# Delta stage: decay sums of the first 16 chains issued one chain ahead of the key products, a second pair of banks for those products, and a denser order for the first batch of block inversions

## The reference, cut to what matters

```python
def step(S, x):
    qt, kt, vt, bt, gt = x
    S = S * jnp.exp(gt)[..., None, None]
    kv = jnp.einsum('bhk,ebhkv->ebhv', kt, S)
    delta = (vt[None] - kv) * bt[..., None]
    S = S + kt[None, :, :, :, None] * delta[..., None, :]
    ot = jnp.einsum('bhk,ebhkv->ebhv', qt * scale, S)
    return (S, ot)
```

## Time and profile before

| | |
|---|---|
| runs of the kernel before | 3254.01, 3258.17, 3269.35 us (median 3258.17) |
| span of the profiled execution | 3278.8 us; no separate device time of that execution is given, so its span stands for it |
| PE busy, DVE, ACT, POOL | 2990.0 (91%), 1674.9 (51%), 1128.2 (34%), 1485.6 (45%) us |
| mean granted TensorE clock | 0.943 of 2.4 GHz |
| delta stage, fronts alone | from 1340 us to 1452 us: 112 us, PE busy 69.91 us of it |
| delta stage, all parts and tail | from 1452 us to about 2000 us, PE busy 523.22 us of 548 |

### The profile page before, as it was taken

How to read it: one execution, slowest core, us unless ns; L and a number is a source line. 1 busy time by engine, 2 the same in 40 slices (tenths; PEclk the granted TensorE clock), 3 DMA queues, 4 the chain that set the end, 5 groups by cost and what they waited for, 6 DMA issues and landing times.

```text
span 3278.8 us, 46022 instructions
## 1 busy us (share of the span) xinstructions
PE 2990.0 (91%) x16081; PEld 1719.2 (52%) x16081; DVE 1674.9 (51%) x3820; ACT 1128.2 (34%) x2501; POOL 1485.6 (45%) x1471
## 2 busy tenths in 40 slices
PE   7999999888999899679999998998999999999828
PEld 3434566577676544357777765444533333444414
DVE  7633266588244432258777632442257777621361
ACT  3312422297122222345666332221034444332201
POOL 0565656498554457333333103554656666300003
PEclk9999999999999899859999778999999999999958
DMA  5400001210111244334554435211167666600404
GB/s 169 138 19 6 13 19 54 68 43 14 42 51 43 69 159 158 125 97 123 135 132 124 123 112 162 83 52 49 30 203 201 205 198 198 160 13 26 175 4 129
DMA packets 275960, 321.36 MB, mean 98 GB/s; under 512 B 155807, under 2 KB 193569, under 8 KB 275732
## 3 DMA queue, kind: packets, MB, share of 16 engines
q1 hardware_dynamic: 219684, 182.57, 18.7%
q0 software_dynamic: 51840, 134.60, 13.6%
q10 hardware_dynamic: 4208, 1.25, 0.2%
HBM read 215.75 MB, written 104.60 MB: 98 GB/s over the span
## 4 chain that ended last, share of the span: by engine, by line
PE 74%; issue 10%; DVE 6%; ACT 4%; POOL 4%; DMA 1%; SPq 0%; ACTq 0%; DVEq 0%; POOLq 0%
PE bank L2700 8%; PE bank L1522 5%; PE bank L2692 5%; PE bank L708 4%; PE bank L1301 3%; PE bank L2363 3%; PE bank L2854 3%; PE bank L2847 3%; PE bank L439 3%; PE bank L731 2%; PE bank L762 2%; PE bank L1117 2%; PE bank L2343 2%; PE bank L1311 2%; PE bank L858 2%
## 5 line engine op out<-in xcount | busy, mean ns | idle before, releaser
L2672 POOL DMA_INDIRECT conv_src<-xn_rows,keep x288 | 272.4, 946 | 176.4 <-DVE conv_msg L2738 111.4
L291 POOL DMA_INDIRECT sorted_bias<-perf_rec,place x256 | 260.2, 1016 | 145.4 <-PE bank L708 90.1
L2700 PE MATMUL bank<-conv_msg,conv_hot 128*128 128x512 f32 x576 | 273.0, 596 | 0.6 <-ACT conv_msg L2719 0.6
L1923 POOL TENSOR_TENSOR delta_dec<-delta_dec,rates_of 128x512 f32<-128x512 f32 x64 | 67.3, 1051 | 338.4 <-ACT delta_dec L1975 338.4
L2738 DVE TENSOR_TENSOR conv_msg<-bank,conv_src 128x512 f32<-128x512 f32 x288 | 185.5, 686 | 47.3 <-PE bank L2692 47.3
L666 POOL DMA_INDIRECT sorted_edge<-rec,place x128 | 127.2, 994 | 141.0 <-PE bank L1362 75.1
L2719 ACT ACTIVATE conv_msg<-conv_msg 128x1024 f32<-128x1024 f32 x144 | 152.0, 1055 | 102.0 <-DVE conv_msg L2738 102.0
L1117 PE MATMUL bank<-bias_prod,bias_hot 128*128 128x256 f32 x640 | 148.2, 387 | 25.2 <-ACT bias_hot L1070 13.1
L2692 PE MATMUL bank<-conv_we,conv_eT 64*128 64x512 f32 x576 | 164.5, 648 | 0.7 <-ACT conv_eT L2716 0.7
L1101 POOL TENSOR_TENSOR bias_prod<-bias_col,bias_rec 128x512 f32<-128x512 f32 x128 | 147.2, 1179 | 16.5 <-PE bank L1117 15.7
L1117 PEld LDWEIGHTS bank<-bias_prod,bias_hot 128*128 128x128 f32 x640 | 120.1, 192 | 53.8 <-issue 28.2
(11 more groups left out here) (502 smaller groups left out, 6756.2 us busy)
## 6 DMA issues: line engine op xcount, KB each, us to landing
keep<-slot_qkv SPq DMA_DIRECT2D x32, 512.0 KB, 3.9
delta_kv<-slot_qkv SPq DMA_DIRECT2D x32, 512.0 KB, 3.9
sorted_edge<-sort_pad SPq DMA_DIRECT2D x8, 1440.0 KB, 7.3
keep<-sorted_edge SPq DMA_DIRECT2D x18, 640.0 KB, 5.2
slot_out<-delta_o SPq DMA_DIRECT2D x64, 128.0 KB, 2.0
conv_src<-xn_rows,keep POOLq DMA_INDIRECT x288, 3.6
X<-in_x SPq DMA_DIRECT2D x4, 1024.0 KB, 10.9
sorted_bias<-perf_rec,place POOLq DMA_INDIRECT x256
```

Of the source, the lines that this page charges most:

```text
L291: POOL.indirect_dma_start(out=sorted_bias, out_offset=bass.IndirectOffsetOnAxis(ap=place[:, 0, c:c + 1], axis=0), in_=rec0[:, c, :], in_of ...
L2672: POOL.indirect_dma_start(out=src[:, n % 4, j, :], out_offset=None, in_=xn_rows, in_offset=bass.IndirectOffsetOnAxis(ap=rec[:, g % 3, k + ...
L2700: a = PE.matmul(bank[n % 2][:, :], hot[:, g % 2, k + j, :], msg[:, q, j, :], start=j == 0, stop=j == 1)
```

## The change

For chains below FIRST = 16 the front is put in another order: mask, turn, kq, low mask, decay, exp and weigh of chain n move ahead by 0.65 to 0.85 positions (transposes and kq by 0.7), gram and BA stay. On PE the order becomes turn(n + 1), gram(n), decay(n + 1); on POOL mask(n + 1), weigh(n). Gram of an odd chain below TWO = 14 goes to banks 6 and 7, so that up to chain 14 gram waits for the BA of two chains back. Transposes stay in banks 4 and 5 up to chain 15. For batch 0 the 30 block columns are spread over 3.0 positions in place of 5.4, its L copy and blocks out come at 13.19 and 13.2, UL in of tile 0 at 13.6 (was 14.6) and of tile 1 at 16.0 (was 16.6; ahead of load kv of tile 1 and of B in of batch 1 at 16.3). From chain 16 on the decay's matmuls get one more wait, for kq of the same chain.

```diff
@@ -1702,7 +1702,7 @@
             MID, MAIN = 16.2, 17.2
-            ALONE = 13
+            ALONE, TWO, FIRST = 16, 14, 16
@@ -1772,10 +1772,16 @@
             plan = []
+            def fronts(n):
+
+                if n < FIRST:
+                    return (("mask", -1.3), ("turn", -0.9), ("kq", -0.8), ("low mask", -0.65), ("decay", -0.4), ("exp", -0.3),
+                            ("weigh", -0.2), ("gram", 0.21), ("BA", 0.72))
+                return (("mask", -0.45), ("turn", -0.2), ("kq", -0.1), ("low mask", 0.08), ("gram", 0.21), ("decay", 0.25),
+                        ("exp", 0.35), ("weigh", 0.45), ("BA", 0.72))
+
             for n in range(NC):
-                for what, at in (("mask", -0.45), ("turn", -0.2), ("kq", -0.1), ("low mask", 0.08), ("gram", 0.21), ("decay", 0.25),
-                                 ("exp", 0.35), ("weigh", 0.45), ("BA", 0.72),
-                                 ("Z", MID + 0.005), ("Z copy", MID + 0.1), ("U", MID + 0.25), ("U copy", MID + 0.35),
+                for what, at in (*fronts(n), ("Z", MID + 0.005), ("Z copy", MID + 0.1), ("U", MID + 0.25), ("U copy", MID + 0.35),
@@ -1784,7 +1790,7 @@
-                plan.append((2 * t + 14.6, "UL in", t))
+                plan.append((2 * t + (14.6 if t >= 2 else 13.6 + 0.4 * t), "UL in", t))
@@ -1794,10 +1800,10 @@
                 for k in range(30, 0, -1):
 
-                    at = 0.75 + 5.4 * (31 - k) / 31
+                    at = 0.75 + (5.4 if q else 3.0) * (31 - k) / 31
                     plan.append((first + int(at) + 0.4 + 0.78 * (at - int(at)), "block column", (q, k)))
-                plan.append((first + 6.33, "L copy", q))
-                plan.append((first + 6.34, "blocks out", q))
+                plan.append((first + (6.33 if q else 5.19), "L copy", q))
+                plan.append((first + (6.34 if q else 5.2), "blocks out", q))
@@ -1809,6 +1815,10 @@
+            def gram_banks(n):
+
+                return bank[6:8] if n < TWO and n % 2 else bank[1:3]
@@ -2037,6 +2047,8 @@
                         PE.wait_ge(*low_masked.at(n + 1))
                         if n >= 1:
                             PE.wait_ge(*decay_ready.at(n))
+                        if n >= ALONE:
+                            PE.wait_ge(*kq_ready.at(n + 1))
@@ -2045,12 +2057,14 @@
                     if what == "gram":
                         PE.wait_ge(*kq_ready.at(n + 1))
-                        if n >= 1:
+                        if n > TWO:
                             PE.wait_ge(*BA_ready.at(n))
+                        elif n >= 2:
+                            PE.wait_ge(*BA_ready.at(n - 1))
...
-                                a = PE.matmul(bank[1 + e][:, 256 * i:256 * i + 256], pair[:, 0, :],
+                                a = PE.matmul(gram_banks(n)[e][:, 256 * i:256 * i + 256], pair[:, 0, :],
@@ -2162,7 +2176,7 @@
-                                                  bank[1 + e][:, :].rearrange("p (i k n) -> p i k n", i=2, k=2),
+                                                  gram_banks(n)[e][:, :].rearrange("p (i k n) -> p i k n", i=2, k=2),
```

## The result

Six runs of the changed kernel had a median of 3242.62 us (3234.17 to 3251.96), six of the kernel before 3256.74 us (3252.40 to 3269.35). The ratio is 0.9941, with a 95% interval from 0.9913 to 0.9969: faster by 0.6%, 14 us by the medians.

What follows compares the result with a forecast made beforehand. No engine full: a loop of dependent steps, 6.62 us a lap, bounds the fronts running alone. Chain 16's gram 28.2 us earlier, less 2.3 for SP, gives 25.9: 3232 us against the 3258.2 median, range 3220 to 3247.

Steps and rivals of the forecast that it cites:

- Part 1: Fronts of chains 0 to 8: a lap of 6.6 us becomes 3.2 at 2.4 GHz, bound by ACT's loop, or 4.3 at 1.2 GHz.
- The clock: PE in chains 0 to 8: idle only 0.6 us a lap, 80% filled, so taken as 2.4 GHz.
- first rival: Chains 0 to 8 at 1.2 GHz too: laps of 4.3 us, gain 17.6 us, 3241 us; chance 20%.
- Part 2: Batch 0 on DVE: masking from 1377.3, then 28.5 us of full DVE; blocks done at 1405.8, a gain of 29.8 us so far.
- Part 3: From the blocks' end to chain 16's gram: 13.5 us, mostly at 1.2 GHz; gram at 1419.3, 28.2 us earlier.
- Part 4: SP's queue: B in of batch 1 goes out 5.9 us behind chain 16's gram, before 3.6; cost 2.3 us, between 0 and 2.3.
- The sum: Whole kernel: 28.2 us gained less 2.3 is 25.9; 3253 us against the profiled execution, 3232 against the median.
- main case: Whole kernel: 25.9 us faster, 3232 us against the median of 3258.2; chance 48%.
- fourth rival: Clock stays at 1.2 GHz from chain 16 on: few slow chains 3243 to 3254 us, 7%; eight or more 3277, slower, 6%.

## Why the prediction was right or wrong

**The lap (Part 1)** came out as summed: 3.22 us against 3.2, ACT's loop as the bound. **The clock** in chains 0 to 8 was 2.4 GHz, as taken (a granted 1.00 from 1348 to 1385 us); the first rival (4.3 us a lap) did not happen. Of the two rules of the Trainium skill's "TensorE: Matmul & The Clock Gate" that I set beside it, the trace agrees with "HAM oscillation — how this bites in real kernels": with gaps of 0.87 us the clock stayed up. Whether the other one holds for transposes by themselves, a lap with 0.60 us of them beside other matmuls does not tell.

**The blocks (Part 2).** Batch 0's masking was due at 1377.3, 1378.4 with the later start of the stage, and came at 1378.48. The columns were mis-sized: 28.5 us was the sum to the blocks' end, 31.7 were measured (1378.48 to 1410.15). The term that failed is the 23.2 us for 60 column instructions, which took 24.9 busy and 1.9 between, 26.8. I took the lengths that they had before, as if they were their own. Two of those 60 had started while POOL was at work, and seven did so now, though POOL had fewer instructions in the stretch (7, before 10). (A slip of 0.2 us: seven laps of 3.2 from 1343.58 end at 1366.0, not 1366.2.)

**To chain 16 (Part 3)** 13.5 us were taken and 12.7 measured. The clock was 1.2 GHz for the decays of 14 and 15 but back at 2.4 GHz for gram(15). Against the start of the stage chain 16's gram came 25.8 us sooner, where I had 28.2.

**What SP gives back (Part 4)** was sized well and placed half right. I said 2.3 us, and from 25.8 at gram(16) the second and ninth steps keep 23.4: 2.4 us. The start of that sum, SP free 9 us behind the blocks, was given without its working; B out(6) went out 8.7 behind L copy's start. But the wait is mostly not SP's order. Moving UL in(1) gave 0.7 us at the second and at the ninth step. Putting r ahead of the waiting masking as well brought this to 4.6 and 1.4, and its two profiles agree. The queue that mattered was DVE's.

**The sum.** 25.9 us forecast, 23.4 measured in two of three profiles at the ninth step and 18.9 in the third, and 14 to 18 in the runs. The first gap is the blocks' later end (3.2, less the 0.8 won in Part 3). The second is the granted clock, in two places: behind PE's idle time for r (up to 4.6 us), and later in the main part, above all in the last 23 chains, where one kernel takes 186 to 214 us at granted clocks of 0.94 and 0.79. The median of the first six runs, 3242.6 us, lies near the 3241 that I gave the first rival, whose mechanism did not happen, and 11 us above the 3232 of my main case: that the time still fell within my range is owed to its width, which was made for that rival, and not to a term for the clock. Whether the changed kernel meets the slow clock more often than the kernel before, or 24 runs are too few to tell, stays open. I gave the fourth rival, a few slow chains in the main part, 7%, as an event of its own. It should have been a term of the sum with a spread, since the earlier trace rows already showed 70 us at 0.50.

The change's three parts are not of one worth. With the denser batch in all of them, the first state step comes at 139.4 us with the old order and one pair of banks, at 110.0 with the second pair alone, at 104.0 with the new order alone, and at 103.2 to 104.2 with both. So either part alone brings most of the gain, the order the larger share, and the banks add next to nothing to it. The denser batch alone costs 10 us, brings nothing at the second and ninth step of the changed kernel, and brings 4.4 and 1.2 us there once r is ahead of the masking.

## What to carry to other kernels

When a hand-written order makes a loop serial, write down every loop that is left after the change (one per engine, one per buffer) with durations from rows: the largest was the new lap to 0.02 us. Look for the step that *waits* on a transfer in each engine's list, and ask which due step is queued behind it; here one position moved on DVE was worth 3.9 us at the second state step, where a whole group of issues moved on SP was worth 0.7. A part that is worth nothing behind a wait can be worth something once the wait is gone: try it again then. Before a gain of half a per cent is read from a few runs or from one pair of profiles, measure it between marks inside the stage that changed.

## What was not expected of the hardware

One kernel, one stretch of 23 chains: 185.7 us at a granted clock of 0.94 and 213.9 at 0.79. In both executions of the kernel before the clock fell at the same place, some 512 us after the stage's first matmul, and the next 17 us ran at 0.50. Then they part, first profile and second:

```profile
1865.30:1920.00 54.70, 52.76 (x392) 37.70 (x391) 24.45 (x81) 12.00 (x34) 2.25 (x4) 0.50 0.28 77
```

```profile
1865.60:1920.00 54.40, 50.64 (x679) 37.11 (x679) 31.28 (x111) 21.07 (x58) 3.87 (x7) 1.00 0.49 139
```

The clock stayed at 1.2 GHz in the first although its PE shows 52.76 us busy of 54.7. What decides between the two was not tried.

POOL's weigh took 2.02 us beside DVE's masking and 1.04 alone, and two column products 0.75 and 0.95 beside POOL and 0.21 to 0.22 alone. Where one of the two grew in the columns of batch 0, it was the one that had started second, on either engine. Moving POOL's work in time changed what DVE's cost.
